# Attention over 49 key positions per block: values weighed one key tile at a time in place of two

## The reference

```
x = L0(x)   # spectral mixing of rows and columns, in float32
q, k, v = proj(wq, bq), proj(wk, bk), proj(wv, bv)         # 8 heads of 16 channels, 3136 tokens
scores = einsum('bhqd,bhkd->bhqk', q, k) / sqrt(16) + bias(|dh| + |dw|)
attn = softmax(scores, axis=-1)
ctx = einsum('bhqk,bhkd->bhqd', attn, v)
resid = ctx @ wo + bo + x
out = layernorm(resid) * ln_gamma + ln_beta
```

## Time and profile before

| | before |
|---|---|
| median of 3 runs | 11227.74 us |
| the profiled execution | 11224.98 us |
| its span | 11223.2 us |
| PE busy | 92% |
| DVE busy | 65% |
| ACT busy | 51% |
| granted TensorE clock, mean | 0.954 |

### The profile page before, as it was taken

One profiled execution on the slowest core, in us unless ns is written; L12 is line 12 of the kernel. 1 busy time (PEld: TensorE's weight loads), 2 busy tenths in 40 slices (PEclk: granted clock), 3 DMA queues, 4 the chain that ended last, 5 costly groups with the idle time before them and its releaser, 6 DMA issues.

```text
span 11223.2 us, 346007 instructions
## 1 busy us (share of the span) xinstructions
PE 10325.6 (92%) x139471; PEld 4470.2 (40%) x139471; DVE 7259.1 (65%) x24584; ACT 5718.0 (51%) x11896; POOL 962.7 (9%) x862
## 2 busy tenths in 40 slices
PE   7888832999999999999999999999999999999998
PEld 4444410344444444444444444444444444444443
DVE  3555511776677667766776677767776777667774
ACT  1111101465556655665566556655665566556655
POOL 0222211000100010001000100010001000110001
PEclk8888855899999999999999999999999999999999
DMA  2434415000100010001000110011001100110000
GB/s 60 88 79 86 92 49 64 5 10 26 30 19 8 25 34 17 9 21 36 19 8 18 32 25 8 19 29 27 10 13 33 29 9 13 28 32 10 9 12 14
DMA packets 443042, 324.26 MB, mean 29 GB/s; under 512 B 75495, under 2 KB 436424, under 8 KB 440520
## 3 DMA queue, kind: packets, MB, share of 16 engines
q1 hardware_dynamic: 433988, 299.91, 11.5%
q10 hardware_dynamic: 7488, 2.77, 0.5%
HBM read 197.66 MB, written 104.87 MB: 27 GB/s over the span
## 4 chain that ended last, share of the span: by engine, by line
PE 71%; issue 6%; DVE 5%; DMA 1%; SPq 0%; ACT 0%; POOL 0%; DVEq 0%; POOLq 0%; ACTq 0%
PE l_ps L967 47%; PE l_ps L1045 20%; DVE summed L1193 2%; PE l_ps L1059 1%; DVE partial L1193 1%; DMA sums_scratch<-ctx_raw 1%; PE l_ps L1075 1%; PE l_ps L1062 0%; PE l_ps L1076 0%; DVE res L1229 0%; PE l_ps L1069 0%; PE l_ps L1056 0%; DVE neg_max L1202 0%; PE l_ps L1064 0%; DVE neg_max L1205 0%
## 5 line engine op out<-in xcount | busy, mean ns | idle before, releaser
L1154 ACT ACTIVATE p<-l_ps 128x448 f32<-128x448 f32 x10976 | 5315.9, 543 | 3668.9 <-PE l_ps L967 3527.8
L1193 DVE CUSTOM_DVE_ANT_0 summed<-l_ps,pair_bias 128x448 f16<-128x448 f32 x9408 | 5435.8, 621 | 2543.8 <-PE l_ps L967 2512.0
L967 PE MATMUL l_ps<-ks,qs 64*64 64x448 f16 x21952 | 4023.5, 363 | 218.5 <-DVE partial L1193 163.7
L967 PE MATMUL l_ps<-low,id 64*64 64x448 f16 x21952 | 3957.5, 357 | 0.4 <-issue 0.4
L967 PE MATMUL l_ps<-high,id 64*64 64x448 f16 x21952 | 3918.7, 353 | 2.2 <-ACT p L1154 1.0
L967 PE MATMUL l_ps<-qs,ks 64*64 64x448 f16 x21952 | 3916.8, 353 | 0.0
L967 PE MATMUL l_ps<-rows,pick_row 64*64 64x448 f16 x21952 | 3869.7, 349 | 0.0
L1045 PE MATMUL l_ps<-p,v 128*32 128x448 f32 x22400 | 2407.2, 545 | 0.3 <-issue 0.3
L967 PEld LDWEIGHTS l_ps<-ks,qs 64*64 64x64 f16 x21952 | 1185.5, 104 | 2337.7 <-DVE partial L1193 2047.4
L967 PEld LDWEIGHTS l_ps<-high,id 64*64 64x64 f16 x21952 | 1199.7, 106 | 1265.4 <-issue 932.0
L967 PEld LDWEIGHTS l_ps<-qs,ks 64*64 64x64 f16 x21952 | 1203.8, 106 | 394.2 <-issue 0.5
(11 more groups left out here) (130 smaller groups left out, 4300.1 us busy)
## 6 DMA issues: line engine op xcount, KB each, us to landing
stacks_scratch<-parts SPq DMA_DIRECT2D x448, 112.0 KB
x<-in_x SPq DMA_DIRECT2D x16, 1568.0 KB
ks<-stacks_scratch SPq DMA_DIRECT2D x32, 784.0 KB, 9.5
qs<-stacks_scratch SPq DMA_DIRECT2D x224, 112.0 KB, 2.7
recip<-inverse_scratch SPq DMA_DIRECT2D x448, 56.0 KB, 2.0
h_scratch<-x SPq DMA_DIRECT2D x8, 1568.0 KB
w_scratch<-x SPq DMA_DIRECT2D x8, 1568.0 KB
mh<-h_scratch SPq DMA_DIRECT2D x64, 196.0 KB
```

The costliest lines, as they stand in the source:

```text
L967: last = nc.tensor.matmul(ps[h * BT:(h + 1) * BT, bank, 0:CH], lhs(part, h), rhs(part, h), start=start, stop=True, skip_group_check=not start)
L1154: nc.scalar.activation(p[unit % PB][:], ps[:, EB + unit % 4, 0:CH], ACT.Exp).then_inc(exp_done, 1)
L1193: nc.vector.tensor_tensor_reduce(summed[unit % 2][:], ps[:, AB + unit % 2, 0:CH], bias.rearrange("p s t -> p (s t)"), 1.0, LOWEST, ALU.add ...
```

## The change

Tiles 0 to 21 were weighed in pairs, at i = 5, 9, ..., 45; tiles 22 and 23 at i = 0 of the next block, and tile 24 at its i = 2. Now one tile is weighed at i = 4, 6, ..., 48 (tiles 0 to 22), tile 23 at i = 0 and tile 24 at i = 2 of the next block. Even tiles are weighed one slot earlier than before, odd ones one slot later. Only PE reads this table; the other engines' lists don't change.

```diff
             n, i = divmod(s, NP)
             if i == 0 and n >= 1:
-                return [(n - 1, 22), (n - 1, 23)]
+                return [(n - 1, 23)]
             if i == 2 and n >= 1:
                 return [(n - 1, 24)]
-            if i % 4 == 1 and i >= 5 and 0 <= n < N:
-                return [(n, i // 4 * 2 - 2), (n, i // 4 * 2 - 1)]
+            if i % 2 == 0 and i >= 4 and 0 <= n < N:
+                return [(n, i // 2 - 2)]
             return []
```

## The result

The changed kernel takes 11424.68 us, the median of 4 runs (11419.76 to 11426.6), against 11227.44 before: a ratio of 1.0175, with a 95% interval of 1.0158 to 1.0193. It is 197 us slower, where 188 were forecast (11415 us). The profiled execution has a span of 11423.1 us.

A forecast was written before the change was run, and what follows sets the result against it. PE bounds the kernel, at DVE's pace from a piece's third slot, with DVE also bounding the second. Blocks +269, normalisation -62, projections -20 gave +187 on 11225.0, thus 11412, or 11415 us as median; range 11335 to 11500.

The forecast's parts named there:

- Stops: PE's halts for weighing: 12 pairs at 1.64 us become 24 singles at 0.89, +1.7 us a block.
- Rival A: A single stop costs 0.82 us, half a pair, when stops are regular: 11227 us, the same; chance 0.05.
- Pieces: PE's runs of slots between stops: 24 of two slots at 2.36 us plus slot 0 at 1.07, +1.3 a block.
- Rival B: DVE no longer runs dry in a shorter stop, so two slots take 2.05 us: 10582 us; chance 0.05.
- The join: DVE reductions at i = 39 hold PE 0.71 us in slot 41; a stop behind slot 40 covers it, -0.7 a block.
- The new wait: At the end of slot 4, weighing tile 0 waits for ACT's context copy: +0.2 us a block, bounds 0 and 0.5.
- Plain block: Attention block without normalisation: 78.1 us before, 80.5 forecast; +2.4 over 112 blocks gives +269 us.
- Block with normalisation: Extra time over a plain block falls from 4.0 to 2.9 us: -1.1 in each of 56 blocks, -62 us.
- Projections: 196 of them behind slots of the blocks; half part a piece of two, -0.1 each on average, -20 us.
- Rivals C and D: C: join's stall stays, copy comes later, 11528 us, chance 0.06. D: order doesn't change what PE does; excluded.
- the covers: PE's stops overlapping DVE's longer jobs: a 0.89 us stop hides the join's 0.71 us wait.

The follow-up runs named there:

- the empty stop: Kernel before, with a one-column matmul in the 128x32 tiling added at the end of 11 slots a block: 11442.28 us, +216 us.
- the pair of runs 128x32 and 64x64: Kernel before, with a one-column matmul added at 11 slots a block, in the weighing's 128x32 tiling (11442.28 us) or the neighbours' 64x64 (11252.38 us).
- the earlier unit: First max_unit of a slot moved from sixth to second of ten groups: 11113.17 us on the kernel before, 11014.05 us on the changed kernel.
- the late half: Kernel before, with only the last six pairs of a block taken apart (tiles 12 to 23 weighed singly): 11251.42 us, ratio 1.0024.
- the early half: Kernel before, with only the first six pairs of a block taken apart (tiles 0 to 11 weighed singly): 11396.18 us, ratio 1.0149.
- the later stops: Changed kernel with its single stops one slot later (tile t at i = 2t + 5; tiles 22 to 24 at i = 0, 1, 2): 11472.51 us.

## Why the prediction was right

*Stops.* +1.7 us a block rested on one row, the 0.89 of tile 24. Every single stop in the stretch of the chain that I read has it. Rival A (0.82) is out; so is the estimate of 0.11 for a stop's two drains from the Trainium skill's TensorE: Matmul & The Clock Gate, since the empty stop measured 0.11 behind it and a gap of 0.11 ahead of it, 0.22. The rule that a change of tiling mode drains the engine (the Trainium skill, TensorEngine Tiling (Array Packing), Key Properties) agrees with the pair of runs 128x32 and 64x64 (0.175 us a place against 0.02), which don't show that it is the drain that costs.

*Pieces.* 24 x 2.36 + 1.07 came as forecast, since DVE is empty at every stop. Rival B needed a DVE that still has a unit when PE goes on; it idled 0.97 us in the stop ahead of slot 39, as against 0.96. The run with the empty stop shows how far off B was. There PE is gone for 0.11 us and DVE idles 0.18 behind it, and the next piece of two takes 2.36 all the same:

```profile
2298.69 0.62 DVE L1196 CUSTOM_DVE_ANT_0 summed<-l_ps,pair_bias 128x448 f16<-128x448 f32 x1 [0.18 <-PE l_ps L967]
```

The loss in the second slot doesn't hang on how long DVE stood idle, but on where in the slots PE makes DVE's units, as the earlier unit showed.

*The join.* Forecast -0.7 a block; the chain has 0.1 left of it. Shown from three sides: the late half keeps the gain, the early half hasn't got it, and the later stops lose it.

*The new wait.* Forecast 0.2 x 112; measured 25.8 us in 111 waits.

*The sums.* Plain block: 80.5 forecast, 80.5 measured. Block with normalisation: 1.3 more than before was forecast (2.4 - 1.1), 83.45 - 82.1 = 1.35 measured. What makes it less than a plain block's 2.4 is mostly one term, and the wait of 0.25 in place of 0.95 in slot 29 is in the timeline: the second `ks,qs` starts 1.03 us into the slot (11038.36 - 11037.33), 0.25 behind its place at 0.78. Projections: the five blocks of an image that have them grew by 4.9 us together in six of seven images, where 2.4 + 4 x 1.3 - 28 x 0.1 = 4.8 follows from the forecast. That is in part luck: the five grew by 2.2, -0.1, -0.2, 1.1 and 1.9 us, where the working, spread evenly, gives 1.8 for the first and 0.7 for each other. In all 187 us were forecast for the profiled execution, and its span grew by 200 (11423.1 - 11223.2). Of the 13 us between, 7 lie in the seven blocks that open a new image, which grew by 2.2 on average and not by 1.3, and 4 outside the first and last L1069; what makes them longer I did not trace. Rivals C and D did not come: the covers held, and the order did what its list says.

What went wrong were expectations behind the prediction: the price of the empty stop (0.11 in place of 0.15 to 0.3) and the gain of the earlier unit (0.02 in place of 0.25 in pieces of four, 0.17 in pieces of two).

## What to carry to other kernels

When one engine is fed through two banks by another that pauses now and then, price the stretches by their length from the chain, not by a mean over them: here slot one cost 0.97, slot two 1.28 (2.36 - 0.97 - 0.11 for the gap), and each after that 1.11. A visit to another tiling cost some 0.22 us here, whatever it did there, so visits should be few, unless they can be laid where another engine has a long job: six extra stops a block cost 170 us in one half (26 of them a wait for a copy that could be moved) and 25 in the other. And a slower schedule may be one reorder away from the better one: with the units placed to suit, single stops beat pairs by 221 us.

## What the runs showed that was not expected

One column in another tiling costs 0.175 us in the end, some eight times the 0.02 of a like matmul in its neighbours' tiling. And the order of ten groups inside a slot, with not one instruction added or removed, was worth more than the change studied: from 10943 to 10589 us by choosing the places of two of the ten by the slot.
